# Even steps for TensorE, a table of score factors and an earlier inverse in the attention part of a transformer layer

## The reference

```python
def attention(h, Wq, bq, Wk, bk, Wv, bv, Wo, bo, gq, gk):       # 32 heads of 128
    q, k, v = h @ Wq + bq, h @ Wk + bk, h @ Wv + bv              # 512 -> 4096
    q, k = rms_norm(q, gq), rms_norm(k, gk)                      # over all 4096
    # per head and batch: softmax(q k^T / sqrt(128)) v, then one product back to 512
    return softmax(q @ k.T * scale) @ v @ Wo + bo

x = x + layernorm(attention(layernorm(x), ...))
x = x + layernorm(x @ W_base.T + b_base + experts(x))            # 8 gated low-rank experts
```

## Time and profile before

| what | before |
| --- | --- |
| time, median of 3 runs | 1098.91 us (1096.74 to 1100.34) |
| time of the profiled execution | 1099.54 us |
| its span | 1097.7 us |
| TensorE busy | 1045.3 us (95%) |
| VectorE busy | 894.4 us (81%) |
| ScalarE busy | 764.7 us (70%) |
| GpSimd busy | 788.7 us (72%) |
| mean granted TensorE clock | 0.995 |
| chain that ended last | PE 60%, DVE 27%, issue 5%, ACT 4% |

### The profile page before, as it was taken

The page is one execution under the profiler, slowest core; times in us unless marked ns, Lnnn a source line. Parts: engine busy times, 40 slices in busy tenths (PEclk is TensorE's granted clock), DMA queues, the critical chain, the costliest instruction groups (busy, mean ns, idle before and its releaser), DMA issues.

```text
span 1097.7 us, 19815 instructions
## 1 busy us (share of the span) xinstructions
PE 1045.3 (95%) x5637; PEld 547.1 (50%) x5637; DVE 894.4 (81%) x1885; ACT 764.7 (70%) x1512; POOL 788.7 (72%) x677
## 2 busy tenths in 40 slices
PE   7999999999999999999999999998999899898997
PEld 4444444444445656645554554554554555453354
DVE  8767887777565878689889898889889888997787
ACT  4666676666557777577776777777777777777756
POOL 2667999999756577565886876777777678567813
PEclk9999999999999999999999999999999999999999
DMA  6678778778854699648767665767666766576612
GB/s 243 172 232 255 233 208 231 217 202 243 195 169 156 164 245 250 191 120 211 174 149 186 178 167 158 182 156 184 163 175 155 189 165 159 138 173 140 160 42 77
DMA packets 312082, 197.86 MB, mean 180 GB/s; under 512 B 275424, under 2 KB 279392, under 8 KB 312032
## 3 DMA queue, kind: packets, MB, share of 16 engines
q1 hardware_dynamic: 304400, 193.71, 65.9%
q10 hardware_dynamic: 7632, 3.57, 1.7%
HBM read 94.45 MB, written 35.68 MB: 119 GB/s over the span
## 4 chain that ended last, share of the span: by engine, by line
PE 60%; DVE 27%; issue 5%; ACT 4%; POOL 1%; DVEq 1%; DMA 1%; SPq 0%; ACTq 0%; POOLq 0%
PE ps L1528 20%; PE ps L1530 20%; PE ps L1529 20%; DVE ps L2496 7%; DVE pair_q L2510 5%; DVE y L2454 4%; DVE wt_lo L2430 3%; ACT pair_q L1268 2%; DVE row_inv L2503 2%; DVE score_down L2326 1%; DVE v_sum L2388 1%; DVE v_second L2388 1%; DVE stats L2009 1%; ACT y L1453 0%; DMA pair_k<-pair_q 0%
## 5 line engine op out<-in xcount | busy, mean ns | idle before, releaser
L1259 ACT ACTIVATE ps<-ps,neg_max 128x512 f32<-128x512 f32 x256 | 168.1, 656 | 75.1 <-DVE ps L2496 75.0
L2510 DVE SCALAR_TENSOR_TENSOR pair_q<-ps,row_inv,pair_q 128x512 f16<-128x512 f32 x256 | 174.5, 745 | 52.3 <-ACT pair_q L1268 52.3
L2496 DVE TENSOR_SCALAR_CACHE_REDUCE ps<-ps,score_down 128x512 f32<-128x512 f32 x256 | 177.5, 756 | 29.8 <-PE ps L1530 24.5
L1528 PE MATMUL ps<-xh,wa_hi 128*128 128x512 f16 x512 | 194.0, 379 | 1.8 <-DVE wa_lo L2114 1.8
L1530 PE MATMUL ps<-xh,wa_lo 128*128 128x512 f16 x512 | 194.0, 379 | 0.0
L1529 PE MATMUL ps<-xl,wa_hi 128*128 128x512 f16 x512 | 194.0, 379 | 0.0
L1268 ACT ACTIVATE pair_q<-ps,row_inv 128x512 f16<-128x512 f32 x256 | 155.1, 689 | 53.8 <-DVE row_inv L2503 53.3
L733 POOL TENSOR_TENSOR acc<-acc,squares 128x512 f32<-128x512 f32 x120 | 159.2, 1347 | 1.6 <-ACT squares L1079 1.6
L937 POOL CAST oth<-o_t 128x512 f16<-128x512 f32 x62 | 38.4, 619 | 129.5 <-ACT o_t L1233 129.2
L1528 PE MATMUL ps<-wo_hi,oth 128*128 128x512 f16 x256 | 97.8, 382 | 33.4 <-DVE y L2454 32.7
L1079 ACT ACTIVATE squares<-ps,q_k_bias,qk_down 128x512 f32<-128x512 f32 x128 | 99.2, 786 | 41.0 <-PE ps L1530 27.2
(11 more groups left out here) (283 smaller groups left out, 2535.5 us busy)
## 6 DMA issues: line engine op xcount, KB each, us to landing
q_k_scratch<-qk_out SPq DMA_DIRECT2D x64, 512.0 KB, 4.9
qk_in<-q_k_scratch SPq DMA_DIRECT2D x64, 512.0 KB, 3.8
wa_stage<-w_qk SPq DMA_DIRECT2D x32, 512.0 KB, 6.3
u_stage<-w_vo SPq DMA_DIRECT2D x32, 512.0 KB, 7.1
wo_stage<-w_vo SPq DMA_DIRECT2D x16, 512.0 KB, 4.4
wv_stage<-w_vo SPq DMA_DIRECT2D x9, 512.0 KB, 4.7
wv_second<-w_vo SPq DMA_DIRECT2D x7, 512.0 KB, 4.5
qk_tops<-qk_top_scratch ACTq DMA_DIRECT2D x27, 128.0 KB, 4.7
```

Of the source, the lines that this page charges most:

```text
L1259: act.activation(ps[:, SCORE + i, :], ps[:, SCORE + i, :], ACT.Exp, bias=neg_max[:, sl, i:i + 1], scale=-1.0, accum_out=row_sum[:, sl, i:i ...
L1528: pe.matmul(outp, lhs[0], rhs[0], start=first, stop=False)
L2496: dve.tensor_scalar(ps[:, SCORE + i, :], ps[:, SCORE + i, :], score_down[:, sl, i:i + 1], None, ALU.mult, ALU.min, accum_out=neg_max[:, sl ...
L2510: dve.scalar_tensor_tensor(out=pair_q[:, 1, i, :], in0=ps[:, SCORE + i, :], scalar=row_inv[:, sl, i:i + 1], in1=pair_q[:, 0, i, :], op0=AL ...
```

## The change

**Products spread 2, 1.5, 1.5, 2 over the steps of a pair.** Before, steps 0, 1 and 3 of a window held two products each and step 2 one. Now `T4` is made half in step 1 and half in step 2. `B21` goes to bank `OB` in place of `VB`, so step 2 waits for `o_t_ready` like the others and, before `attend`, for VectorE to have read `OB`. VectorE adds `B21`'s result into `v_first` early in step 2 and the sum with `T4` late in step 2. ScalarE's high halves of the two values move to late in step 2 and early in step 3, GpSimd's low halves both to step 3.

**Inverses between the sums of y.** `inverses` stands between the first and the second sum of y, and its second instruction also writes out an accumulator (`row_seen`), which nothing reads.

**Score factors in a table.** `scores_down` is gone from the steps. `others_down` makes the factors of heads 2 to 31 in two instructions after step 3, and `maxima` picks its column by a register.

**Weights' low halves last.** `B11`'s and `B22`'s low halves move from early to late in a step; `B11` from step (2, par 0) to (1, par 0), `B22` from (2, par 1) to (1, par 1). ScalarE's high half of `T4` moves from (3, par 0) to (0, par 1) and that of `B21` from (0, par 1) to (1, par 1). In steps 0 and 3 of a window ScalarE makes `k_hi` behind the high halves of the probabilities in place of ahead of them.

```diff
-            def low_alpha(w, b, i):
-                pool.wait_ge(alpha_high, 2 * w + 2 - i)
-                pool.tensor_tensor(v_tiles(vl, b, i, 0), v_sum[:, :, :], v_tiles(vh, b, i, 0),
-                                   ALU.subtract).then_inc(alpha_ready, 1)
+            def low_alpha(w, b):
+                for i, src in ((0, v_first), (1, v_sum)):
+                    pool.wait_ge(alpha_high, 2 * w + 1 + i)
+                    pool.tensor_tensor(v_tiles(vl, b, i, 0), src[:, :, :], v_tiles(vh, b, i, 0),
+                                       ALU.subtract).then_inc(alpha_ready, 1)
...
-                if window is not None and s >= 2:
-                    low_alpha(*window, 3 - s)
+                if window is not None and s == 3:
+                    low_alpha(*window)
...
-                if prepare:
+                early = prepare and (window is None or s in (1, 2))
+                if early:
                     high_k((s + 2) % 4, n + 2)
                 for i in range(TB):
                     high_halves(n, sl, i)
+                if prepare and not early:
+                    high_k((s + 2) % 4, n + 2)
...
                     if (s, par) == (3, 0):
                         high_term(quad, 3, T3, wv_second[:, 0:2, :])
+                    if (s, par) == (0, 1):
                         high_term(quad, 4, T4, wt_4[:, :, :])
-                    if (s, par) == (0, 1):
+                    if (s, par) == (1, 1):
                         high_block(B21, wv_stage[:, 2:4, :])
-                    if (s, par) == (1, 1):
                         high_block(B22, wv_second[:, 2:4, :])
                         high_block(T1, wt_1[:, :, :])
...
-                    product(a(1, 1), T4, b, VB)
+                    product(a(1, 1), T4, b, VB, (0,))
                 if s == 2:
+                    product(a(1, 1), T4, b, VB, (1,))
                     block_ready(5)
-                    pe.wait_ge(v_added, 5 * w + 3)
-                    product(a(0, 1), B21, b, VB)
+                    product(a(0, 1), B21, b, OB)
...
-            def scores_down(n, h, sl, b):
+            def scores_down(b, h):
 
-                dve.tensor_scalar(score_down[:, sl, :], rms[:, NT * b:NT * b + TB + 1], exp_scale[:, bass.ds(h, 1)],
+                dve.tensor_scalar(score_down[:, b, h, :], rms[:, NT * b:NT * b + TB], exp_scale[:, h:h + 1],
                                   None, ALU.mult).then_inc(score_down_ready, 1)
+
+            def others_down(b):
+
+
+                dve.tensor_tensor(score_down[:, b, 2:HEADS, :],
+                                  exp_scale[:, 2:HEADS].unsqueeze(2).broadcast_to([P, HEADS - 2, TB]),
+                                  rms[:, NT * b:NT * b + TB].unsqueeze(1).broadcast_to([P, HEADS - 2, TB]),
+                                  ALU.mult).then_inc(score_down_ready, 1)
...
             def low_early(quad, s, par):
-                if (s, par) == (2, 0):
-                    low_block(quad, 1, B11, wv_stage[:, 0:2, :])
                 if (s, par) == (0, 1):
                     low_block(quad, 3, T3, wv_second[:, 0:2, :])
-                if (s, par) == (2, 1):
-                    low_block(quad, 6, B22, wv_second[:, 2:4, :])
 
             def low_late(quad, s, par):
+                if (s, par) == (1, 0):
+                    low_block(quad, 1, B11, wv_stage[:, 0:2, :])
...
                 if (s, par) == (1, 1):
                     low_block(quad, 5, B21, wv_stage[:, 2:4, :])
+                    low_block(quad, 6, B22, wv_second[:, 2:4, :])
...
                 for i in range(TB):
                     dve.wait_ge(scores_ready, 4 * n + i + 1)
-                    dve.tensor_scalar(ps[:, SCORE + i, :], ps[:, SCORE + i, :], score_down[:, sl, i:i + 1], None,
+                    dve.tensor_scalar(ps[:, SCORE + i, :], ps[:, SCORE + i, :],
+                                      score_down[:, b, bass.ds(h, 1), i:i + 1].rearrange("p a t -> p (a t)"), None,
                                       ALU.mult, ALU.min, accum_out=neg_max[:, sl, i:i + 1]).then_inc(max_ready, 1)
...
-                dve.tensor_scalar(row_inv[:, sl, :], row_rec[:, sl, :], P_UP, None,
-                                  ALU.mult).then_inc(inv_ready, 1)
+                dve.tensor_scalar(row_inv[:, sl, :], row_rec[:, sl, :], P_UP, None, ALU.mult, ALU.min,
+                                  accum_out=row_seen[:, sl:sl + 1]).then_inc(inv_ready, 1)
...
-                maxima(n, sl)
+                maxima(n, 2 * p + sl, s // 2, sl)
                 if rows:
 
-                    add_rows((s - 1) % 4, n - 1, to)
+                    add_row((s - 1) % 4, n - 1, 0, to)
+                inverses(n, sl)
+                if rows:
+                    add_row((s - 1) % 4, n - 1, 1, to)
                 if window is not None:
                     values_early(*window, s)
                 if quad is not None:
                     low_early(quad, s, par)
-                inverses(n, sl)
```

More of the change, by code:

```diff
@@ L147, in build @@
         row_inv = sb("row_inv", [P, 2, TB + 1])
-        score_down = sb("score_down", [P, 2, TB + 1])
+        row_seen = sb("row_seen", [P, 2 * TB + 2])
         exp_scale = sb("exp_scale", [P, HEADS])
@@ L286, in build @@
         v_fourth = sb("v_fourth", [P, 2, WIDE])
+        score_down = sb("score_down", [P, 2, HEADS, TB])
         v_joint = qk_tops[:, :, :, :].rearrange("p a q w -> p a (q w)")
@@ L1193, in values_early @@
                     act.wait_ge(v_part, 7 * w + 1)
+                    if not first_window(w):
+                        act.sem_inc(begun, 1)
+                        act.wait_ge(alpha_ready, 2 * w - 1)
                     act.activation(v_first[:, :, :], bank_of_values(OB), ACT.Copy, scale=V_DOWN).then_inc(v_saved, 1)
-                if s >= 2:
-                    act.wait_ge(v_added, 5 * w + 1 + s)
-                    act.activation(v_tiles(vh, b, 3 - s, 0), v_sum[:, :, :], ACT.Copy).then_inc(alpha_high, 1)
+                if s == 3:
+                    high_alpha(w, b, 1, v_sum)
             def values_late(w, b, s):
+                if s == 2:
+                    high_alpha(w, b, 0, v_first)
                 if s == 3:
@@ L1715, in values, with product @@
                 v_item(pair % 2, 2 * ((item - 1) % 4), VB)
-            def product(left, block, b, bank):
-                for t in range(2):
+            def product(left, block, b, bank, tiles=(0, 1)):
+                for t in tiles:
                     for k, half in enumerate(left(b, t)):
@@ L2513, in low_halves, with add_row, step @@
                                          op1=ALU.subtract).then_inc(low_ready, 1)
-            def add_rows(s, n, to=None):
-                for k in range(2):
-                    add_y(2 * n - 5 + k, 2 * ((s + 1) % 4) + k, YB + k, to).then_inc(y_added, 1)
-            def step(p, s, par, items=(), rows=True, down=True, to=None, window=None, quad=None):
+            def add_row(s, n, k, to=None):
+                add_y(2 * n - 5 + k, 2 * ((s + 1) % 4) + k, YB + k, to).then_inc(y_added, 1)
+            def step(p, s, par, items=(), rows=True, to=None, window=None, quad=None):
                 n = 4 * p + s
                 sl = s % 2
-                maxima(n, sl)
+                maxima(n, 2 * p + sl, s // 2, sl)
                 if rows:
-                    add_rows((s - 1) % 4, n - 1, to)
+                    add_row((s - 1) % 4, n - 1, 0, to)
+                inverses(n, sl)
+                if rows:
+                    add_row((s - 1) % 4, n - 1, 1, to)
                 if window is not None:
@@ L2541, in step @@
                     low_late(quad, s, par)
-                if down:
-                    scores_down(n + 1, 2 * p + (s + 1) % 2 + (2 if s == 3 else 0), 1 - sl, (s + 1) % 4 // 2)
-            maxima(0, 0)
+            dve.wait_ge(score_down_ready, 1)
+            maxima(0, 0, 0, 0)
             inverses(0, 0)
@@ L2555, in _ @@
             low_wv(1, 0)
-            maxima(1, 1)
+            dve.wait_ge(score_down_ready, 2)
+            maxima(1, 1, 0, 1)
             inverses(1, 1)
@@ L2565, in _ @@
             dve.wait_ge(rms_ready, 2)
-            scores_down(2, 0, 0, 1)
+            scores_down(1, 0)
             first_low_k(1)
             low_wo(0)
-            maxima(2, 0)
+            dve.wait_ge(score_down_ready, 3)
+            maxima(2, 0, 1, 0)
             low_wo(1)
@@ L2574, in _ @@
                 low_halves(2, 0, i)
-            scores_down(3, 1, 1, 1)
+            scores_down(1, 1)
+            dve.wait_ge(score_down_ready, 4)
             step(0, 3, 0, items=(5,), rows=False)
+            others_down(0)
+            others_down(1)
+            dve.wait_ge(score_down_ready, 6)
             dve.wait_ge(y_down_ready, 1)
@@ L2729, in _ @@
             step(PAIRS - 1, 2, 1)
-            maxima(N + 1, 1)
+            maxima(N + 1, HEADS - 1, 1, 1)
             added = 2 * N - 6
```

37 lines of the change are left out of this document (16 added, 21 removed).

## The result

The changed kernel takes 1067.27 us, the median of 4 runs (1064.62 to 1068.70), against 1099.62 of the kernel before (4 runs). The ratio is 0.9708, 95% interval [0.9679, 0.9736]. The profiled execution takes 1068.7 us with a span of 1066.9; forecast were 1070.6 us and a range of 1064 to 1083.

What follows compares the result with a forecast made beforehand. TensorE's waits for VectorE's sum of y were taken as the bound: 37.7 us less 5.8 left is 31.9, less 3.6 for margins a gain of 28.3, so 1071.2 us profiled, 1070.6 median; range 1064 to 1083.

Steps and rivals of the forecast that it cites:

- The bound: TensorE's waits for VectorE's sum of y; without them an eight-step loop turn falls from 86.4 to 80.5 us at best.
- The addition of 0.16 to each wait: TensorE's waits at `rows` are larger than shown, by 0.16 us each: 32.7 us in 31 waits becomes 37.7.
- S: Start of a step's scores on TensorE; first maxima at S + 0.85, TensorE going on behind the first sum at S + 4.34.
- the margin: Steps 1 and 2: punctual first sum at S + 4.44, with 0.1 for the separate wait, against `rows` at S + 4.55.
- the removed instructions: Table: 60 of 64 small VectorE instructions, mean 485 ns, 29 us of work, counting only where VectorE was late.
- The rival on the accumulator form: Accumulator form held up beside GpSimd, too: second sum 0.3 later, 7 us lost in steps 1 and 2, 1078 us; chance 0.06.
- The row of 1.81 for `T3`: Step 0 of an odd pair: the early low half of `T3` on VectorE can take 1.81 us.
- the tight place: Step 0 of an odd pair: `T4`'s low half waits for ScalarE's high half, ending M + 9.9 to 10.4 against 10.4.
- the 3.6 us taken off for margins: Taken off the gain: 0.1 for each of 24 steps with 1.5 products and 0.2 for six odd pairs.
- The waits without products: Waits in steps without products that stay: 1.84 at 478.6 and at 1015.4, about 2.1 at 1004.1; 5.8 us left.
- the 0.2: Loss allowed for the late low half of `T4` in step 0 of each of six odd pairs.
- the rival "Slower": Separate wait costs each of the maxima its own time; at 0.5 us, 29 us more in five turns, 1126; chance 0.03.

Runs made afterwards that it cites:

- e1: Changed kernel with value products 2, 2, 1, 2 as before, with their value sums and halves: 1073.84 us, ratio to before 0.9761.
- e8: Changed kernel plus one small unneeded VectorE operation between maxima and first sum of y in every step: 1070.85 us, ratio to before 0.9730.
- e5: Kernel before with the new spread of products alone, plus the changed kernel's order of ScalarE's halves: 1103.78 us, ratio 1.0034.
- e6: Kernel before with the inverses between the two sums of y, in the form with accumulator: 1077.88 us, ratio 0.9793.
- e10: Kernel before with the inverses between the two sums of y, in their plain form: 1081.34 us, ratio 0.9832.
- e4b: Changed kernel with inverses behind both sums of y again, accumulator form kept, one added VectorE wait: 1072.11 us, ratio to before 0.9745.
- e3: Changed kernel with the inverses' second operation in plain form, without accumulator, at its new place: 1074.23 us, ratio to before 0.9768.
- e11: Kernel before with the inverses at their old place behind both sums, in the form with accumulator: 1090.56 us, ratio 0.9920.
- e2: Changed kernel without the table, each step computing the next step's score factors as before: 1071.92 us, ratio to before 0.9744.
- e7: Changed kernel with the low halves of B11 and B22 early again, as before: 1067.09 us, ratio to before 0.9697.
- e13: Kernel before with the score-factor table alone, plus ScalarE's new order of halves and one more VectorE wait: 1087.41 us, ratio 0.9890.

## Why the prediction was right

**The bound.** It was right. The turn was given as 80.5 from counts of matmuls and measured at 80.52. The addition of 0.16 to each wait is borne out by the turns of both kernels, by e1, and by e8, where waits of 0.13 us have no mark.

**Products.** The separate wait costs 0.15, not 0.1 (maxima at S + 1.00 for 0.85 before). The first sum ends at S + 4.44, `rows` start at S + 4.55. With the 0.06 that TensorE takes behind a sum, the margin was 0.05 where I had 0.1. It still held, and e8 spent it. What I did not say is that this edit, with ScalarE's order, takes nothing off a turn until the others are made (e5), and 1.2 us as the last one (e1).

**Table.** It was right in direction. It gives 2.5 us a turn alone (ScalarE's order included) and 0.8 as the last part. So it is right that the removed instructions count only where VectorE was late, but VectorE was late nearly everywhere.

**Inverses.** This was right, and it is the largest part (e6, 22 of 32 us). The place works by ScalarE, which starts its high halves sooner (e10, e4b); the form by not being held up beside GpSimd (e3, e11). The rival on the accumulator form has fallen: 157 to 160 ns in all 64, with GpSimd at work or not. The Trainium skill (SBUF — State Buffer, Who interferes with whom) exempts this form, and the trace agrees.

**Low halves.** The row of 1.81 for `T3` that I feared is 0.85 in the changed kernel (734.84 in VectorE's timeline), and VectorE stands idle for 0.42 at the end of the odd step 0. The high half of `T4` came in time there, but no more than that: with the inverses late, VectorE waits 0.48 for it (e4b). It is indeed the tight place: each part taken from VectorE's gains overruns most there (e2, e3, e4b). That the low halves of B11 and B22 are late is worth nothing (e7).

**The sum.** The term mis-sized is the 3.6 us taken off for margins: it was 0 in the loop. Without it the sum gives 1067.0 for the median, and 1099.54 - 31.9 = 1067.6 for the traced execution. The waits without products are 5.1 + 3 x 0.16 = 5.6 against 5.8 assumed; the first in the last pair shrank from 3.10 to 1.70. The execution traced also paid 1.6 more for a DMA near 390 and reached its step n = 1 0.9 later, both outside what was costed. That would make 1070.1 or, with the 0.2, 1069.9, and 1068.7 was measured: some 1.2 us were won outside the loop where the sum has nothing, and no run places them. So the mechanism and the loop's share (29.1 us measured, 5 x 5.8 = 29.0 costed) are no luck, but that the median of 1067.27 comes so near to 1067.0 in part is. In the rival "Slower", 29 us on some 1099 make 1128, not 1126.

**What the parts are worth.** Alone on the kernel before, place, form, table and products take 3.22 + 2.16 + 2.49 + 0.01 = 7.9 us off a turn; each as the last one added, they take 0.93 + 1.48 + 0.83 + 1.20 = 4.4; the whole is 5.89. The last two of the first row have the 0.48 of ScalarE's order against them. The first three shorten one chain, VectorE's through ScalarE, and none can bring a turn below TensorE's own; place and form together take 4.10 off (e6), not 5.38, and leave the turn at 82.31, so they overlap even above that. The fourth moves TensorE's turn, from 81.7 to 80.5. ScalarE's new order by itself was not tested.

## What to carry to other kernels

Before costing an edit to the engine that waits, look whether the engine it waits for has a gap in any step: if every gap there is only the price of a wait instruction, the order of the waiting engine can win little yet. Put the small result that another engine waits for ahead of one's own long work, and price a small instruction by its rows in the late steps, not by its mean. When the bound has moved, parts that are measured one by one no longer add up; measure each from both ends. When work moves from one step to another, look in the trace who waits for it there, in the small kernels of the experiments too.

## What the runs showed of the hardware

A 128x5 multiplication from SBUF on VectorE takes 0.17 us with GpSimd idle (364.92 in the kernel before) and up to 1.22 beside GpSimd, where it ended 0.03 us after GpSimd's instruction (e3; 1.02 in e13). It is not held each time: at 426.91 in the kernel before it took 0.17 in the midst of a multiplication on GpSimd (426.03, 1.56 long). The same with an accumulator takes 0.16 in each of 64, with GpSimd at work or not, and the accumulator's read of 0.08 costs hardly more: the next instruction starts 0.02 behind it (734.15 and 734.17 in the changed kernel). How long the plain form is held depends on what it falls beside: with 0.5 us taken out of each step, its mean rose by 0.11 us (e13). A wait of TensorE of 0.13 us has no mark in the list of waits, yet in four steps of eight it made each turn 0.53 us longer (e8).
